# A selective-scan block on one core: the D term moves from a PE matmul to an addition on VectorE

## What is computed

```python
xr, gate = jnp.split(x @ W_in.T, 2, axis=-1)        # 2 x 1024 channels
xr = xr + t_emb[:, None, :]
xc = silu(depthwise_conv_4_taps(xr) + b_conv)
xn = layernorm(xc) * ln_g + ln_b
Bm, Cm, dt = jnp.split(xn @ W_xproj.T, 3, axis=-1)  # 16 states each
...
def step(h, inputs):
    ad, bd, xt, ct = inputs
    h = jnp.clip(h * ad[:, :, None] + bd[:, :, None] * xt[:, None, :], -10.0, 10.0)
    yt = jnp.einsum('bd,bdh->bh', ct, h)
    return (h, yt)
y = ys.transpose(1, 0, 2) + D * xn
return x + y * silu(gate) @ W_out.T
```

## Time and profile before

| | us |
|---|---|
| median of 3 runs | 2062.3 (2061.71 to 2063.79) |
| the profiled execution | 2062.99 |
| its span, first to last instruction | 2061.2 |
| PE busy | 1871.3 (91%) |
| GpSimd busy | 1746.4 (85%) |
| VectorE busy | 1602.5 (78%) |
| ScalarE busy | 1379.5 (67%) |

### The profile page before, as it was taken

One profiled execution on the slowest core, in us unless ns is written; L12 is line 12 of the kernel. 1 busy time (PEld: TensorE's weight loads), 2 busy tenths in 40 slices (PEclk: granted clock), 3 DMA queues, 4 the chain that ended last, 5 costly groups with the idle time before them and its releaser, 6 DMA issues.

```text
span 2061.2 us, 46097 instructions
## 1 busy us (share of the span) xinstructions
PE 1871.3 (91%) x16368; PEld 1417.4 (69%) x16368; DVE 1602.5 (78%) x2045; ACT 1379.5 (67%) x3462; POOL 1746.4 (85%) x1444
## 2 busy tenths in 40 slices
PE   5589999999999999999999999999999999999988
PEld 5466776767776766776776776676776676777655
DVE  3387787878887878887888887877887787878786
ACT  4577666777666677667677666777766776766653
POOL 1388888899888889988889988889988889988896
PEclk9699999999999999999999999999999999999999
DMA  5222222222222222222222222232222222222221
GB/s 177 58 56 60 70 63 64 73 59 68 75 58 67 68 64 66 73 58 71 65 72 61 69 58 73 62 75 62 67 57 76 62 77 59 67 62 72 57 68 31
DMA packets 168068, 139.14 MB, mean 68 GB/s; under 512 B 100704, under 2 KB 137968, under 8 KB 163168
## 3 DMA queue, kind: packets, MB, share of 16 engines
q1 hardware_dynamic: 167840, 136.20, 24.8%
HBM read 62.07 MB, written 9.31 MB: 35 GB/s over the span
## 4 chain that ended last, share of the span: by engine, by line
PE 52%; ACT 17%; issue 15%; DVE 10%; SPq 2%; POOL 2%; DMA 1%; DVEq 0%; ACTq 0%; POOLq 0%
PE ps_y L599 11%; PE ps_job L516 8%; PE ps_job L482 7%; DVE ks L997 6%; PE ps_fill L563 6%; PE ps_fill L572 6%; PE ps_job L495 4%; ACT tap L759 3%; ACT low L801 3%; PE ps_y L579 3%; PE ps_job L489 3%; ACT xh L697 2%; PE ps_job L486 2%; ACT lend L779 1%; ACT gate L691 1%
## 5 line engine op out<-in xcount | busy, mean ns | idle before, releaser
L997 DVE TENSOR_TENSOR_SCAN ks<-low,ps_fill 128x512 f32<-128x512 f32 x1024 | 1211.3, 1208 | 267.6 <-PE ps_fill L572 267.2
L1095 POOL TENSOR_TENSOR prod<-ks,crep 128x512 f32<-128x512 f32 x1024 | 1285.6, 1273 | 157.3 <-DVE ks L997 131.0
L801 ACT COPY low<-ps_fill 128x512 f32<-128x512 f32 x1024 | 584.5, 580 | 518.0 <-PE ps_fill L563 515.4
L599 PE MATMUL ps_y<-c_sb,prod 128*128 128x128 f32 x4096 | 610.2, 274 | 1.8 <-POOL prod L1095 1.0
L599 PEld LDWEIGHTS ps_y<-c_sb,prod 128*128 128x128 f32 x4096 | 458.6, 141 | 80.3 <-issue 43.7
L563 PEld LDWEIGHTS ps_fill<-ts,xs 128*128 128x128 f16 x4096 | 314.4, 98 | 176.5 <-issue 9.9
L572 PE MATMUL ps_fill<-spans,pick 128*128 128x512 f16 x1024 | 390.2, 381 | 46.8 <-ACT low L801 46.8
L563 PE MATMUL ps_fill<-ts,xs 128*128 128x128 f16 x4096 | 397.1, 220 | 13.2 <-DMA xs<-h 7.3
L759 ACT ACTIVATE tap<-xr,cols_sb 128x128 f32<-128x128 f32 x768 | 251.8, 393 | 0.0
L477 PE MATMUL ps_job<-x,w_in 128*128 128x128 f16 x3072 | 215.4, 221 | 10.3 <-POOL x L1065 7.8
L482 PE MATMUL ps_job<-w_in,x 128*128 128x512 f16 x768 | 203.3, 381 | 21.3 <-ACT gate L691 21.3
(11 more groups left out here) (123 smaller groups left out, 2003.1 us busy)
## 6 DMA issues: line engine op xcount, KB each, us to landing
crep<-c_dram SPq DMA_DIRECT2D x32, 1024.0 KB, 4.8
xs<-xh SPq DMA_DIRECT2D x256, 64.0 KB, 2.0
xs<-xl SPq DMA_DIRECT2D x224, 64.0 KB, 2.0
xf<-in_xT SPq DMA_DIRECT2D x32, 256.0 KB, 2.8
res<-in_x SPq DMA_DIRECT2D x32, 256.0 KB, 2.7
out_dram<-res SPq DMA_DIRECT2D x32, 256.0 KB, 2.3
ts<-tth SPq DMA_DIRECT2D x128, 32.0 KB
ts<-tth SPq DMA_DIRECT2D x128, 31.0 KB
```

The costliest lines, as they stand in the source:

```text
L599: last = mm(ps_y[:, cut], prod[:, (TILES * k + s) % HOLD, e, :], ident, start=False, stop=(u % 4 == 3 and q == 3 and e == QN - 1), is_tran ...
L801: copy(low[:, (TILES * k + s) % RING], ps_fill[:, (TILES * k + s) % RING]).then_inc(sem["low_copied"], 1)
L997: nc.vector.tensor_tensor_scan(ks[:, u % 2, QN * q:QN * (q + 1)].rearrange("d n t -> d (n t)"), low[:, g % RING], ps_fill[:, g % RING], 0. ...
L1095: tt(prod[:, g % HOLD], ks[:, u % 2, part], crep[:, p, part], ALU.mult).then_inc(sem["weighed"], 1)
```

## The change

The identity matmuls of D * xn leave PE. `gated` has two VectorE instructions in place of one: it adds `xd` to `ps_y` on the way to the job bank (and with that releases `ps_y`, by a new semaphore `y_summed`, for which `base` now waits), then multiplies by the gate within the job bank. GpSimd makes `xd` in two halves, the second of them in the buffer of half 1's 16-bit parts (now `y1`), for which it waits until the transposes of the pass before have landed. ScalarE's silu waits for `y_summed` at its first half only.

```diff
-        xd = xc
-        y16 = [gate[:, 0:BANK].bitcast(H).rearrange("t (a d) -> t a d", a=2), sb("y16", [P, 2, BANK], H)[:]]
+        y1 = sb("y1", [P, BANK])
+        y16 = [half.bitcast(H).rearrange("t (a d) -> t a d", a=2) for half in (gate[:, 0:BANK], y1[:])]
+        xd = [xc[:, 0:BANK], y1[:]]
...
             def base(k, p, i):
-                since(pe, "y_gated", 2 * k + i)
+                since(pe, "y_summed", 2 * k + i)
                 mm(ps_y[:], mT[:, p], xn[:, p, half], start=True, stop=False)
-
-            def skip(k, p, i):
-
-                if i == 0:
-                    pe.wait_ge(sem["xd_done"], k + 1)
-                last = mm(ps_y[:], ident, xd[:, i * BANK:(i + 1) * BANK], start=False, stop=False)
-                if i == 1:
-                    last.then_inc(sem["xd_used"], 1)
...
-                if s in (3 * NQ, 4 * NQ):
-                    skip(k, p, s // NQ - 3)
...
                     since(act, "xa", k + 2)
-                    since(act, "xd_used", k + 1)
+                    if i == 0:
+                        since(act, "y_summed", 2 * k + 1)
...
                 dve.wait_ge(sem["flipped"], TILES * k + TILES // 2 * (i + 1))
+                dve.wait_ge(sem["xd_done"], 2 * k + i + 1)
+                bank_free(dve, k + i, [job[2:4] for job in JOBS].index(("yT", i)))
+                tt(bank("yT", i), ps_y[:], xd[i], ALU.add).then_inc(sem["y_summed"], 1)
                 dve.wait_ge(sem["gate_taken"], 2 * k + i + 1)
-                bank_free(dve, k + i, [job[2:4] for job in JOBS].index(("yT", i)))
-                tt(bank("yT", i), ps_y[:], gate[:, half], ALU.mult).then_inc(sem["y_gated"], 1)
+                dve.wait_ge(sem["y_summed"], 2 * k + i + 1)
+                tt(bank("yT", i), bank("yT", i), gate[:, half], ALU.mult).then_inc(sem["y_gated"], 1)
...
-                        tt(xd[:], xn[:, p], row_d[:], ALU.mult).then_inc(sem["xd_done"], 1)
+                        since(pool, "yT_in1", N_YT * k)
+                        for i in range(2):
+                            half = slice(i * BANK, (i + 1) * BANK)
+                            tt(xd[i], xn[:, p, half], row_d[:, half], ALU.mult).then_inc(sem["xd_done"], 1)
```

## The result

The changed kernel takes 2057.68 us (median; 2056.79 to 2059.64), the kernel before on the same chip 2063.76 (2061.1 to 2064.72): a ratio of 0.9977 [0.9969, 0.9985], 0.23% or some 5 us faster. The profiled execution took 2057.47 us, its span 2055.7.

The account below looks back on a forecast made before the run. PE was busiest (91%, 52% of the chain), but ScalarE and VectorE set one stretch of each pass. 29 passes at 0.22 us, 6.4 us, less 0.3 and 0.75, gave 5.3 us: 2057.0 us, range 2051.5 to 2063.

Parts of the forecast that it names:

- Where the matmuls lie: On PE, each identity matmul takes 0.86 us: half 0's, before waits, worth nothing; half 1's worth 0.86 us a pass.
- The rival that PE's work counts: Second matmul gained in full on PE, 2036 us, or both, 2009 us; chance 0.08.
- D: Delay of the end of VectorE's gate multiplication, hence of ScalarE's cast of y: 0.75 us, bounds 0.70 to 0.83.
- The pair doesn't overlap: On VectorE, the multiplication waits for the addition's result; the rival, overlap with 0.59 us delay, gave 2052 us, chance 0.10.
- ScalarE's chain: From the cast of y: 3.61 us to the `low` copy, 1.08 to the silu's end, 0.55 to PE's next item.
- The new wait: PE's tile-19 transposes wait for the conv bank that ScalarE's silu frees (`xc`), about 0.4 us in every pass.
- 0.97 - D: Gain of a pass at PE's item behind tile 19, at most 0.86 us; 0.22 us with D = 0.75.
- The stall for yT_taken: PE reaches the output job's bank wait about when VectorE's low part ends; covered by a bigger stall, no size given.
- Base's release: VectorE's addition releases PE's next base matmul at the multiplication's old place; PE's 1.51 us wait stays as before.
- half 1's pair on VectorE: The added multiplication, 0.75 us, is hidden in VectorE's 2.25 us idle in the first half of a pass.
- GpSimd's split product: 0.15 us more a pass on GpSimd, off the usual path; its wait for transposes has 3 us left, costing nothing.
- The ends: Outside usual passes: 0.75 us in the serial last pass, and 0.3 us in all where PE waits for transfers.

## Why the prediction was right

I forecast 2057.0 us and 0.26%; measured were 2057.68 us and 0.23%. The cause is the forecast's own, shown by experiment at each term of a pass. The absolute time is hit better than it deserves: the kernel before stood at 2062.3 us in the forecast and at 2063.76 beside the changed one.

- **Where the matmuls lie.** Half 0's worth nothing: the kernel without it took 1.0004 of the time, with PE's wait for `low` in its place. The forecast took the 1.10 us wait for the first one behind that matmul; a wait of 0.39 us stands ahead of it and is the one that grew. Half 1's worth 0.84 us: 60.58 us a pass without it. The rival that PE's work counts (2036 or 2009 us) is thereby right for one matmul in a kernel without D, and wrong here. I first held a busy share of 91% against 52% of the chain; neither would have told the two apart, only the stretch did. The Trainium skill, Perfetto Trace Analysis, section "Identifying the Most-Contended Engine", has the engine with the highest occupancy optimised first; taken as a rule for each piece of its work, which the page does not claim, it would fail here, since one of two identical pieces was worth 0.84 us a pass and the other 0.
- **D.** Taken as 0.75, bounds 0.70 to 0.83; it was 0.80. The op took 0.70 as foreseen, the gap was 0.10 in place of 0.05. I had two gaps in the rows, 0.03 and 0.13, and explained the larger one away with PE's release; but that came at 1029.13, when the first instruction ended, and so explains nothing of it. Since a swap of waits alone moves the gap from 0.11 to 0.04, it matters how an instruction waits, and the larger row was the nearer one: there, too, the wait for the neighbour is one that the instruction does not carry itself (see the last section).
- **The pair doesn't overlap.** The multiplication starts 0.77 us after the addition, not 0.59. The Trainium skill, VectorE: DVE Perf Modes, section "The DRAIN you can't avoid", says of eight copies in a row that a semaphore after each costs nothing extra. I took it for a rule on every pair and made 0.59 of it. The section gives no such figure and has the next operation wait until the one before has left the pipeline, unless nothing holds it, so the 0.59 was my inference and not the page's. The traces have 0.71 us from start to start at best for this pair, and 0.59 where the next operation doesn't need the result.
- **ScalarE's chain.** Of the 3.61, 1.08 and 0.55 us of the forecast the trace has 3.60, 1.08 and 0.54. The new wait is there from the third pass on, 0.36 us long and 0.41 with the slower start behind it, where the forecast had about 0.4. With D = 0.80 the formula 0.97 - D gives 0.17 us a pass; measured 0.18. Nearly doubling D moved the pass by 0.75 us for a cast 0.73 us later.
- **The stall for yT_taken.** I said it is covered by the bigger wait. It is 0.27 us long, and it is covered in the sense that it adds nothing while the conv's wait stands behind it; that much is argued, since no run moves it alone. But once the conv's wait is moved it is what remains, 60.87 us against 60.58. The forecast named it and gave it no size.
- **What costs nothing.** Base's release (1.51 us, unchanged), half 1's pair on VectorE (idle 1.80 us left of 2.25), GpSimd's split product (2.46 us, no wait for transposes): all as forecast.
- **The ends.** 29 passes at 0.18 are 5.2 us; the two profiled executions differ by 5.5. I had 6.4 for the passes less 1.05 for the ends and transfers. Of the ends, two terms can be read: in the last pass the low part of y starts 2.15 us after the last reading of `ps_y`, before 1.35, so D stands there in full with 0.80 us; PE's three waits for a transfer rose by 0.1 us in all (7.3 to 7.4), not by 0.3. (Two slips of the sum on the way: three transfers at 0.15 us are 0.45, not 0.3, and at D = 0.83 the sum is 2.9, not 3.0.) The rest moves by more than that. Against the execution before, the changed one is 0.35 us behind at the second base, 1.17 us ahead at the third, 7.26 at the base near 1954 us and 5.87 at the last. The two jumps, 1.5 and 1.2 us, each have a stretch of the clock beside them, told below, so the sum's agreement within 0.7 us is in part luck.

The largest thing missed stands outside the sum: the terms 0 for half 0's matmul and 0.97 - D together say that half 0's part of the change only loses. I had both numbers and did not draw the conclusion that half of the change would be worth 27 us.

## What to carry to other kernels

Price each half of a symmetric change by itself, in its own stretch: here one half gains 0.84 us a pass, the other gains nothing and delays the engine on which the first one's gain depends, and the gain left is a fifth. When work is taken off an engine, look up its next waits in program order and subtract what the change makes late; two waits for banks, each put a part or two ahead of the first write, ate 0.68 of 0.86 us, and moving them gave it back (0.9886 against 0.9977). And where one instruction waits for a neighbour on its own engine, the order of its waits is worth a try.

## What the runs showed of the hardware

- **A few longer passes.** Now and then a pass is 0.35 us longer, with nothing in the program to mark it. In the kernel before, this one ends at 1861.31, 61.77 us after the base before it, and PE's usual 1.51 us for VectorE is 1.86:

```profile
1861.31 1.12 PE L579 MATMUL ps_y<-xn,mT 128*128 128x512 f32 x2 [1.86 <-DVE ps_job L985]
```

  The execution before had four of them (near 386, 878, 1370 and 1861 us, so 492 us apart), the one after one of this size and one of 0.14 us; about 0.9 us of the difference between the two traces is from this. They are not scattered by chance: the kernel before, the two without a matmul and the one with only the waits moved have their four at the same passes, and the changed kernel in both its executions, the swapped one and the two with waits moved in it, on at least two chips, have their one at the same pass. Each time it is the same VectorE instruction (L976, writing `xl`) that starts 0.41 us after the separate record of its last wait has ended and not the usual 0.06. What holds it stays open.
- **The clock, at the ends and in the middle.** Near 157 us in the kernel before and near 2015 us after, PE had waited for something else and its granted clock then stood lower for most of 4 us. Each row is a stretch: its bounds, its length, busy us and instructions of PE, PEld, VectorE, ScalarE and GpSimd, then PE's clock as a share of full speed, DMA share, GB/s. The kernel before first, then the one after:

```profile
157.00:161.00 4.00, 4.00 (x24) 3.40 (x25) 2.02 (x3) 2.66 (x4) 2.33 (x2) 0.57 0.17 63
```

```profile
2015.00:2019.00 4.00, 3.12 (x15) 2.45 (x16) 3.21 (x3) 0.71 (x2) 4.00 (x4) 0.59 0.01 2
```

  A share of 0.57 or 0.59 is a stretch spent mostly at 1.2 GHz, the lower of the two levels. Ahead of the first PE had waited 2.54 us for a transfer, ahead of the second 1.77 us for GpSimd. The length of the wait alone doesn't tell: at the first place the changed kernel waited 2.06 us in this execution, without such a stretch, and 2.07 us when it ran again, with one; the kernel without half 0's matmul waited 2.52 us there without one. The two stretches go with 1.5 and 1.2 us between the executions; a third one, near 1961 us in the changed kernel, with next to nothing.

  Five of the twelve profiled executions have such a stretch in the middle of the run too, each time right behind a wait of PE that one of the longer passes has made 1.86 to 1.87 us long. This is the kernel without half 0's matmul:

```profile
1369.00:1373.00 4.00, 4.00 (x16) 2.87 (x14) 2.02 (x3) 2.94 (x10) 2.85 (x3) 0.59 0.15 38
```

  Its pass took 63.11 us in place of 61.44. The kernel before had the same wait at 1369.67 us, and its clock stayed at full speed. Each stretch thus moves an execution by up to 1.7 us, in either direction between two kernels, a third of the effect that was measured here. Where passes repeat, their distance tells more than the total.
